# A fused decoder layer on one core: one hand-written order for everything after the last score tile

## What is computed

```python
x = _layernorm(x + _L0_attn_ref(x, ...), axis=-1)
x = _layernorm(x + _L0_xattn_ref(x, ctx_768, ...), axis=-1)
x = _layernorm(x + _L0_ffn_ref(x, ...), axis=-1)
...
# attention: rms norm and rope on q and k, tanh cap of 50, causal softmax, 16 heads on 4 kv heads
scores = jnp.tanh(scores.astype(jnp.float32) / CAP) * CAP
...
# second sublayer: attention over 32 context rows, a film, a long convolution, a film, a feed-forward, a norm
c_t = jnp.einsum('btg,bgd->btd', attn_mean, V)
y = jnp.fft.irfft(xf * Kf.T[None], n=n, axis=1)[:, :L]
h = jax.nn.gelu(h @ W1 + b1, approximate=False) @ W2 + b2
...
# third: two shared experts for all tokens, and the two best of eight by a router
shared = shared.mean(axis=0)
topk_vals, topk_idx = jax.lax.top_k(gates, TOP_K)
moe = jnp.einsum('te,etd->td', w, y)
return (shared + moe).reshape(B, L, D)
```

## Time and profile before

| | us |
|---|---|
| median of 3 runs | 712.1 (711.7 to 712.75) |
| the profiled execution's own time | 709.74 |
| its span, first to last instruction | 707.9 |
| TensorE busy | 479.5, 68% of the span |
| VectorE / ScalarE / GpSimd busy | 341.3 / 329.7 / 249.9 |
| score tiles end | about 392 |
| first scatter of batch 1 issued | 428.5 |
| first transposed block of group 1 | 616.55 |

### The profile page before, as it was taken

The page is one execution under the profiler, slowest core; times in us unless marked ns, Lnnn a source line. Parts: engine busy times, 40 slices in busy tenths (PEclk is TensorE's granted clock), DMA queues, the critical chain, the costliest instruction groups (busy, mean ns, idle before and its releaser), DMA issues.

```text
span 707.9 us, 9570 instructions
## 1 busy us (share of the span) xinstructions
PE 479.5 (68%) x3361; PEld 336.8 (48%) x3361; DVE 341.3 (48%) x1004; ACT 329.7 (47%) x557; POOL 249.9 (35%) x298
## 2 busy tenths in 40 slices
PE   3543552477758867877568788399796679676960
PEld 2221220246326733556235566366694576466960
DVE  4887658726273464845533563313542333024224
ACT  1078685666654775565647225043052343233430
POOL 2304236412350162533431526702434535413441
PEclk9975675669588997989669889699898989888895
DMA  3600000197100000000000101625044303376642
GB/s 105 195 1 0 1 1 0 32 183 155 66 24 39 1 15 1 1 1 1 0 0 1 36 26 39 186 102 168 1 125 145 120 27 98 108 256 209 211 145 85
DMA packets 39713, 51.53 MB, mean 73 GB/s; under 512 B 8561, under 2 KB 28818, under 8 KB 39666
## 3 DMA queue, kind: packets, MB, share of 16 engines
q1 hardware_dynamic: 37170, 45.78, 22.7%
q0 software_dynamic: 2496, 5.15, 2.1%
HBM read 41.25 MB, written 13.86 MB: 78 GB/s over the span
## 4 chain that ended last, share of the span: by engine, by line
PE 40%; DVE 22%; POOL 12%; ACT 9%; issue 7%; SPq 5%; DMA 3%; POOLq 0%; DVEq 0%; ACTq 0%
PE ring_s L871 5%; SPq L436 5%; PE bank_o L690 5%; POOL expert_rows L1187 4%; PE bank_d L779 4%; PE bank_o L901 3%; PE ring_s L675 3%; PE ring_u L766 3%; ACT probs L986 2%; PE ring_u L758 2%; PE bank_r L567 2%; POOL rstd L1099 2%; PE bank_o L887 2%; ACT probs L993 2%; PE bank_d L808 2%
## 5 line engine op out<-in xcount | busy, mean ns | idle before, releaser
L986 ACT ACTIVATE probs<-ring_s 128x512 f32<-128x512 f32 (+1 forms) x192 | 94.6, 523 | 77.8 <-PE ring_s L675 76.2
L675 PE MATMUL ring_s<-qT,kT 128*128 128x512 bf16 (+3 forms) x256 | 72.4, 348 | 78.7 <-ACT probs L986 64.2
L1137 POOL TENSOR_SCALAR_AFFINE_SELECT probs<-probs 128x256 f32<-128x256 f32 (+1 forms) x96 | 51.9, 571 | 156.2 <-ACT probs L993 156.2
L1042 ACT ACTIVATE g_ring<-ring_s,w_blk 128x128 f32<-128x128 f32 x184 | 52.3, 369 | 66.4 <-PE ring_s L871 66.4
L1198 POOL DMA_INDIRECT token_pairs<-y_blk,x_blk x46 | 45.5, 988 | 102.6 <-DVE y_blk L1725 100.2
L675 PEld LDWEIGHTS ring_s<-qT,kT 128*128 128x128 bf16 x256 | 23.4, 104 | 119.6 <-ACT probs L986 87.8
L993 ACT ACTIVATE probs<-probs 128x2560 f32<-128x2560 f32 x32 | 74.8, 2336 | 2.7 <-ACT probs L986 0.4
L871 PE MATMUL ring_s<-xT_blk,w_blk 128*128 128x128 f32 x368 | 53.7, 293 | 11.8 <-DVE xT_blk L1718 7.7
L690 PE MATMUL bank_o<-probs,vv 128*32 128x128 f32 (+3 forms) x512 | 55.1, 589 | 5.4 <-POOL probs L1137 5.4
L871 PEld LDWEIGHTS ring_s<-xT_blk,w_blk 128*128 128x128 f32 x368 | 48.9, 207 | 15.2 <-issue 12.4
L1099 POOL TENSOR_TENSOR rstd<-var_eps,neg_half 128x4 f32<-128x4 f32 x24 | 24.8, 1034 | 83.6 <-DVE var_eps L1433 83.6
(11 more groups left out here) (358 smaller groups left out, 970.5 us busy)
## 6 DMA issues: line engine op xcount, KB each, us to landing
w_blk<-expert_pack SPq DMA_DIRECT2D x46, 514.0 KB, 4.7
expert_pack<-in_L_ffn_W SPq DMA_DIRECT2D x16, 256.0 KB, 9.8
expert_rows<-blank SPq DMA_DIRECT2D x6, 520.0 KB, 3.1
x_blk<-expert_rows SPq DMA_DIRECT2D x10, 260.0 KB, 4.3
y_pair<-token_pairs SPq DMA_DIRECT2D x4, 512.0 KB, 4.5
x_in<-in_x SPq DMA_DIRECT2D x4, 256.0 KB, 3.1
cosm<-in_c_cos SPq DMA_DIRECT2D x1, 1024.0 KB, 6.4
sin_fwd<-in_c_sin_fwd SPq DMA_DIRECT2D x1, 1024.0 KB, 9.2
```

What stands on the lines that cost most here:

```text
L675: last = mm(bank[:, c:c + w], kT[:, r, p // 2, P * j:P * (j + 1)], qT[:, p, P * j:SEQ], start=True, stop=True)
L986: f(probs[:, pair % PAIRS_HELD, BASE[n]:BASE[n] + WIDTH[n]], ring_s[k % 2][:, 0:WIDTH[n]], ACT.Tanh, scale=1.0 / (CAP * float(np.sqrt(np.f ...
L1042: last = f(g_ring[:, s % RING, P * n:P * (n + 1)], ring_s[s % 2][:, P * n:P * (n + 1)], ACT.Gelu, bias=w_blk[:, k % SLOTS, HID + n:HID + n ...
L1137: last = g.affine_select(out=v, in_=v, compare_op=ALU.is_ge, fill=0.0, base=0, pattern=[[0, v.shape[1]], [1, P]], channel_multiplier=-1)
```

## The change

Everything up to the last score tile keeps its order. Behind it the grid walk is replaced by one list, `DRAIN`, of 173 entries (name, batch and part, or unit number), which every engine's program walks. `UNIT_AT` is gone; the list holds the calls 0 to 42 itself, so the plain loop behind still starts at 43. Three steps are cut smaller, with the same instructions: `route` into route (to the choice) and weights, `place` into place (to rank_read) and rows (table and rows), and `scatter` into eight parts of two DMAs, of which the first keeps the waits. In the main walk the parts stand next to each other where the whole stood. The parts of scatter for batches 0 and 2 issue nothing.

```diff
--- before.py
+++ after.py
@@ -74,8 +74,8 @@
     (2, 0, 0, "dft", 7), (2, 0, 1, "spectrum"), (3, 0, 5, "x2_norm"), (3, 1, 0, "x2"), (2, 1, 0, "conv", 0),
     (2, 1, 1, "conv", 1), (2, 1, 2, "conv", 2), (2, 1, 3, "conv", 3), (2, 1, 4, "conv", 4), (2, 1, 5, "conv", 5),
     (2, 2, 0, "conv", 6), (2, 2, 1, "conv", 7), (3, 1, 1, "x2T"), (3, 1, 3, "gates"), (1, 1, 4, "yT"),
-    (3, 2, 1, "gates_exp"), (1, 2, 0, "proj"), (3, 2, 1, "route"), (1, 2, 3, "x1"), (2, 2, 4, "shape_out"),
-    (3, 2, 4, "rank"), (3, 2, 5, "place"), (3, 3, 0, "scatter"), (1, 3, 1, "x1T"), (1, 3, 3, "x_norm"), (1, 3, 2, "scores"), (1, 3, 3, "xn"),
+    (3, 2, 1, "gates_exp"), (1, 2, 0, "proj"), (3, 2, 1, "route"), (3, 2, 1, "weights"), (1, 2, 3, "x1"), (2, 2, 4, "shape_out"),
+    (3, 2, 4, "rank"), (3, 2, 5, "place"), (3, 2, 5, "rows"), *[(3, 3, 0, "scatter", n) for n in range(8)], (1, 3, 1, "x1T"), (1, 3, 3, "x_norm"), (1, 3, 2, "scores"), (1, 3, 3, "xn"),
     (-1, *XT_AT, "xT"), (2, 3, 4, "h_norm"), (1, 3, 3, "cross_exp"), (-1, *QKV_AT, "qkv"), (2, 4, 1, "h"),
     (1, 4, 1, "soften"), (1, 4, 3, "attnT"), (2, 4, 4, "hT"), (-1, 5, 2, "rms"), (2, 5, 0, "up", 0),
     (2, 5, 1, "up", 1), (2, 5, 2, "up", 2), (2, 5, 3, "up", 3), (-1, 5, 2, "rope"), (2, 5, 1, "gelu"),
@@ -122,11 +122,31 @@
 SHARED = [s for s, u in enumerate(UNITS) if u[0] == "s"]
 BACK = 3
 POSITIONS = len(UNITS) + BACK
-UNIT_AT = [(B, p, n) for p in range(2, NPAIR) for n in range(NF)][2:2 + 6 * HC]
-UNIT_AT += [(B + 1, 2, 3), (B + 1, 2, 5), *[(B + 1, 3, n) for n in range(NF)], (B + 1, 7, 2), (B + 1, 7, 5)]
-UNIT_AT += [(B + 2, 0, 0), (B + 2, 0, 1)]
-UNIT_AT += [(B + 2, p, n) for p in range(3) for n in range(NF)][10:17]
-EARLY = len(UNIT_AT)
+DRAIN = [
+    ("dft", 2, 7), ("spectrum", 2), ("x2_norm", 1), ("close", 3), ("x2", 1), ("conv", 2, 0), ("tokens", 3), ("x2T", 1),
+    ("conv", 2, 1), ("gates", 1), ("gates_exp", 1), ("conv", 2, 2), ("conv", 2, 3), ("route", 1), ("unit", 0), ("yT", 3),
+    ("weights", 1), ("conv", 2, 4), ("unit", 1), ("rank", 1), ("unit", 2), ("proj", 3), ("place", 1), ("unit", 3), ("rows", 1),
+    ("x1", 3), ("conv", 2, 5), ("conv", 2, 6), ("conv", 2, 7), ("unit", 4), ("scatter", 1, 0), ("unit", 5), ("shape_out", 2),
+    ("x1T", 3), ("unit", 6), ("x_norm", 3), ("scores", 3), ("xn", 3), ("unit", 7), ("cross_exp", 3), ("h_norm", 2), ("unit", 8),
+    ("soften", 3), ("h", 2), ("unit", 9), ("unit", 10), ("scatter", 1, 1), ("scatter", 1, 2), ("attnT", 3), ("unit", 11),
+    ("hT", 2), ("unit", 12), ("up", 2, 0), ("scatter", 1, 3), ("scatter", 1, 4), ("up", 2, 1), ("gelu", 2), ("up", 2, 2),
+    ("up", 2, 3), ("down", 2, 0), ("scatter", 1, 5), ("film", 3, 0), ("film", 3, 1), ("film", 3, 2), ("film", 3, 3),
+    ("scatter", 1, 6), ("down", 2, 1), ("modulate", 3), ("down", 2, 2), ("down", 2, 3), ("scatter", 1, 7), ("dft", 3, 0),
+    ("ff_out", 2), ("dft", 3, 1), ("ffT", 2), ("ff_norm", 2), ("unit", 13), ("dft", 3, 2), ("dft", 3, 3), ("dft", 3, 4),
+    ("x2_norm", 2), ("dft", 3, 5), ("dft", 3, 6), ("unit", 14), ("dft", 3, 7), ("unit", 15), ("spectrum", 3), ("unit", 16),
+    ("conv", 3, 0), ("conv", 3, 1), ("x2", 2), ("conv", 3, 2), ("x2T", 2), ("conv", 3, 3), ("gates", 2), ("conv", 3, 4),
+    ("conv", 3, 5), ("gates_exp", 2), ("conv", 3, 6), ("route", 2), ("conv", 3, 7), ("shape_out", 3), ("unit", 17), ("weights", 2),
+    ("h_norm", 3), ("unit", 18), ("h", 3), ("unit", 19), ("rank", 2), ("place", 2), ("unit", 20), ("hT", 3), ("rows", 2),
+    ("unit", 21), ("up", 3, 0), ("unit", 22), ("up", 3, 1), ("gelu", 3), ("up", 3, 2), ("scatter", 2, 0), ("up", 3, 3),
+    ("down", 3, 0), ("scatter", 2, 1), ("down", 3, 1), ("down", 3, 2), ("down", 3, 3), ("scatter", 2, 2), ("ff_out", 3),
+    ("scatter", 2, 3), ("unit", 23), ("ffT", 3), ("unit", 24), ("ff_norm", 3), ("unit", 25), ("scatter", 2, 4), ("unit", 26),
+    ("x2_norm", 3), ("unit", 27), ("x2", 3), ("unit", 28), ("x2T", 3), ("unit", 29), ("gates", 3), ("gates_exp", 3), ("unit", 30),
+    ("route", 3), ("unit", 31), ("weights", 3), ("unit", 32), ("scatter", 2, 5), ("rank", 3), ("place", 3), ("unit", 33),
+    ("rows", 3), ("scatter", 2, 6), ("scatter", 2, 7), ("scatter", 3, 0), ("unit", 34), ("unit", 35), ("scatter", 3, 1),
+    ("unit", 36), ("unit", 37), ("unit", 38), ("unit", 39), ("scatter", 3, 2), ("unit", 40), ("unit", 41), ("scatter", 3, 3),
+    ("scatter", 3, 4), ("scatter", 3, 5), ("scatter", 3, 6), ("scatter", 3, 7), ("unit", 42),
+]
+EARLY = sum(name == "unit" for name, *_ in DRAIN)
 FINAL_AT = {BLOCKS[NB] + 4: 0, BLOCKS[NB] + 9: 1}
 STORE_BEFORE = {NB + 12: 0, NB + 17: 1}
 
@@ -156,10 +176,6 @@
         if (q, m) == (p, n) and 0 <= b < B and name in parts:
             parts[name](b, *part)
 
-    for k, at in enumerate(UNIT_AT):
-        if at == (i, p, n) and "unit" in parts:
-            parts["unit"](k)
-
 
 def iterate(parts, first, fill, close, tokens):
 
@@ -167,18 +183,23 @@
                        ("fold3",), ("fold4",), ("rope", 0), ("parts", 0), ("steps",)):
         if name in parts:
             parts[name](*row)
-    for i in range(B + 3):
-        if i < B:
-            first(i)
+    for i in range(B):
+        first(i)
         for p in range(NPAIR):
             for n in range(NF):
-                if i < B:
-                    fill(i, p, n)
-                if n == TOKENS_AT and i <= B:
+                fill(i, p, n)
+                if n == TOKENS_AT:
                     tokens(i, p)
                 run(parts, i, p, n)
-            if i <= B:
-                close(i, p)
+            close(i, p)
+
+    for name, *which in DRAIN:
+        if name == "close":
+            close(B, 0)
+        elif name == "tokens":
+            tokens(B, 1)
+        elif name in parts:
+            parts[name](*which)
 
 
 def build(nc, t, out):
@@ -1176,16 +1197,16 @@
                     last = g.tensor_copy(x_rows[:, k, NT * (b % GB):NT * (b % GB + 1), 0:D], x2[:, b, :].rearrange("p (j d) -> p j d", j=NT))
                 last.then_inc(rows_copied, 1)
 
-            def scatter(b):
+            def scatter(b, j):
 
                 if b % GB < GB - 1:
                     return
-                pool.wait_ge(blanked, 16 * GROUPS * FILL_TURNS)
-                pool.wait_ge(rows_ready, b // GB + 1)
-                for j in range(GB * NT):
-                    for k in range(2):
-                        g.indirect_dma_start(out=rows_dram, out_offset=bass.IndirectOffsetOnAxis(ap=rows_i[:, k, j:j + 1], axis=0),
-                                             in_=x_rows[:, k, j, :], in_offset=None).then_inc(scattered[b // GB], 16)
+                if j == 0:
+                    pool.wait_ge(blanked, 16 * GROUPS * FILL_TURNS)
+                    pool.wait_ge(rows_ready, b // GB + 1)
+                for k in range(2):
+                    g.indirect_dma_start(out=rows_dram, out_offset=bass.IndirectOffsetOnAxis(ap=rows_i[:, k, j:j + 1], axis=0),
+                                         in_=x_rows[:, k, j, :], in_offset=None).then_inc(scattered[b // GB], 16)
 
             def unit(at):
                 s = at - BACK
@@ -1648,6 +1669,10 @@
                 one(tt(cmp_a[:, :, :, :], cmp_a[:, :, :, :], cmp_b[:, :, :, :], ALU.add))
                 one(v.tensor_reduce(chosen, cmp_a[:, :, :, :], AX, ALU.add))
                 ts(chosen_bf[:, :, :], chosen, 2.0, None, ALU.is_lt).then_inc(chosen_ready, 1)
+
+            def weights(b):
+
+                chosen, w_tok = of_batch(chosen_g, b), of_batch(w_tok_g, b)
                 dve.wait_ge(chosen_ready, b + 1)
                 one(ts(chosen, chosen, 2.0, None, ALU.is_lt))
                 dve.wait_ge(gates_exp, b + 1)
@@ -1665,6 +1690,9 @@
                        held[:, :].unsqueeze(1).broadcast_to([P, NT, NE]), ALU.add))
                 op(ts(wT[0:NT * NE, b, :], bank_r[0:NT * NE, P:2 * P], float(NSH), None, ALU.mult))
                 tt(held[:, :], held[:, :], bank_r[:, 64 + NT * NE:64 + NT * NE + NE], ALU.add).then_inc(rank_read, 1)
+
+            def rows(b):
+
                 if b % GB == GB - 1:
                     dve.wait_ge(rank_read, b + 1)
                     block_table(b // GB)
@@ -1767,7 +1795,7 @@
                      "proj": proj, "scores": scores, "x_norm": x_norm, "soften": soften, "film": film_step,
                      "modulate": modulate, "spectrum": spectrum, "shape_out": shape_out, "hT": hT_step,
                      "ffT": ffT_step, "ff_norm": ff_norm, "x2": x2_step, "gates": gates_step,
-                     "route": route, "place": place, "unit": unit, "x1": x1_step, "xn": xn_step,
+                     "route": route, "weights": weights, "place": place, "rows": rows, "unit": unit, "x1": x1_step, "xn": xn_step,
                      "h_norm": h_norm, "h": h_step, "x2_norm": x2_norm}, first, nothing, close, tokens)
             moe()
 
```

## The result

The changed kernel takes 678.3 us in the median of four executions (674.9 to 679.9), the kernel before 712.1: a ratio of 0.953, interval 0.950 to 0.956. Forecast were 671.5 and a range of 652 to 694. The profiled execution took 677.41 with a span of 675.6, so 1.8 lie around it, as before.

The account below looks back on a forecast made before the run. TensorE's waits, 51.5 us between 394.2 and 616.55, bound that stretch, not throughput. Group 1's first matmul comes 39.1 earlier, clock gives 1.5: span 667.3, plus 1.84 around it and 2.36 to the median: 671.5 us, range 652 to 694.

Parts of the forecast that it names:

- case C: Rival: the list packs better than reckoned, most waits and their slow clock halve: 659 us; chance 0.17.
- Item 3: VectorE makes the row table ahead of x1(3), outlasting TensorE's work beside it: a new wait of 2.1 us.
- Item 4: Only two scatter DMAs precede batch 2's norm on GpSimd: 1.0 us left of 12.3; the other 14 cost nothing.
- Item 6: Batch 3's spectrum stands behind batch 2's second norm on VectorE: TensorE waits 2.5 us, before it was 5.0.
- Item 9: Batch 3's rows step on VectorE now stands between block units 33 and 34: TensorE waits 3.1 us.
- Item 10: Batch 3's scatter shares GpSimd with y scatters of units 34 to 41; the third y buffer is late twice: 2.0 us.
- The clock: TensorE's slow clock after three waits that pass 2 us, beside the first wait: 2.4 us each, 7.2 together.
- The scatter's path: From the end of batch 3's rows to unit 55's first matmul: 42.3 us, ending at 583.5, against 582.2 on TensorE's path.
- The rule against the change: VectorE beside the chunked scatter may lock GpSimd out: up to 8 us, time up to 679; the sum took 0.
- B: Rival: the chains of batches 2 and 3 (spectrum, h norm, output norm) keep their waits: 688 us; chance 0.23.
- D: Rival: the list only moves waits and the time stays near 712 us; chance 0.03.
- E: Rival: slower, as block units wait for the three y buffers; 718 us if landing plus queue is 10.5; chance 0.07.

Follow-up runs that it names:

- e1: The changed kernel run once more, unaltered, beside the kernel before: 660.46 us, ratio 0.927.
- e12: The changed kernel with batch 1's last three scatter chunks behind batch 2's feed-forward norm, and batch 2's second norm behind batch 3's spectrum: 672.21 us.
- e6: The kernel before, order kept, with only batch 1's scatter cut into eight chunks: 717.39 us, ratio 1.010 to the kernel before.

## Why the prediction was right or wrong

**The result as a whole.** 678.3 stands in the forecast's own case, 662 to 681, 6.8 above its middle; on the chip of e1 the kernel is 11.0 below it, in case C. So the middle was hit by neither. The forecast had one number for a kernel that has two, by chip. That the first measurement fell into the forecast's own case is in part luck: without late starts the sum is 11.0 too high, and the late starts, which it doesn't have, add 17.9.

**The sum.** Unit 55's transpose was forecast at 580.3 = 394.2 + 156.3 + 22.6 + 7.2. On the chip of e1 it comes at 572.6: its waits add up to 17.2, 5.4 less, and TensorE is busy 161.0 from 394.2 on, so 4.7 of slow clock, 2.5 less. In the first measurement it comes at 590.2: waits 28.6, 6.0 more, busy 167.1, so 10.8 of slow clock, 3.6 more. Both shares of slow clock are what is left when 156.3 is taken off, so they can't confirm it. By the granted clock e1 lost about 3.4 us (next but one paragraph), so 1.3 of its 161.0 is not placed: the constant held to about that.

**Item by item,** e1 first, then the first measurement where it differs. Item 1 (values): 5.2 forecast, 5.2. Item 2: 0.7, measured 0.3. Item 3 (rows ahead of x1): 2.1, measured 0.35. The row table took 4.7 us in e1 (from the block counts at 417.85 to 422.55), as the second of the two in the earlier trace rows did, and I had taken the first, 6.3. That is 1.6 of the 1.75 us. Item 4 (hT of batch 2): 1.0, measured 0.4, and the 14 remaining DMAs hidden, as said; e12 shows with how little to spare. Item 5: 0.5, nothing. Item 6 (spectrum): 2.5, measured 1.8, and 5.2 where the add of ffT starts late. Item 7: 1.0, measured 0.5 + 0.2. Item 8 (output norm beside blocks): 4.5, measured 0.7 + 1.7 + 0.8 + 1.1 = 4.3. Item 9 (rows of batch 3): 3.1, measured 3.45. Item 10 (y ring): 2.0, measured 0; in the first measurement 1.2, behind a late start. So items 3, 6 and 10 are most of what was mis-sized, 4.5 of the 5.4 us, all in one direction: where I could not see a queue's slack I wrote a small wait. (Two waits of 0.3, at 406.08 and 432.50, are in no item.) Item 10 was also where rule and row differed. The Trainium skill, "DMA: Bandwidth & Descriptors", section "Anatomy of one DMA — SWDGE (gpsimd) path", gives 2.15 as an estimate and so no wait. The row itself was read too simply: the view of token_pairs mixes the y scatters with the loads of y_pair, and the view of y_blk, which has the scatters alone, gives 2.2/3.8/5.1 before the change. In e1 the last landing report of a y scatter comes 2.2 to 5.7 us after its issue, 4.1 in the median of 46, and there was no wait all the same. So the skill's page would have given the right wait, by a landing that only the shortest of these come near. What kept the third buffer free was not traced; VectorE must come back to it later than I had it.

**The clock.** I charged three waits with 2.4 each. Apart from the values' stretch (0.51 from 399.7 to 404.3 in e1, 0.56 before), two stretches of e1 have a granted clock under 1: 0.87 from 467 to 480, behind the spectrum's 1.8, and 0.79 from 533 to 541, behind the 3.45 at rows. The block unit behind rows takes 3.6 us instead of 1.9, so 1.7 lost, and the inverse transforms behind the spectrum lose as much. So the price of 2.4 was some 0.7 too high, and the third wait (item 3) wasn't there.

**The scatter's path.** Rows(3) was done 0.7 ahead of the first scatter DMA, at 537.9 in the first measurement (541.2 forecast) and at 533.5 in e1. From there to unit 55's matmul e1 took 575.15 - 533.5 = 41.7, where I had 42.3. In e1 the weights behind that path do hold TensorE by 0.4 (the first block's have landed at 575.06, the matmul starts at 575.15), so the two paths are as near to each other as the forecast said.

**The step that failed** is the last sentence of the forecast: "a step on a queue that I took as free, ScalarE's above all, which I found nowhere last". In the first measurement four shared units between 560.63 and 578.26 take 17.6 us instead of 4 x 1.75 = 7.0, for ScalarE, 10.6 us, and the late add costs 3.4 in front of the spectrum, with some slow clock behind it. But it is not ScalarE's queue that is full. Its activations are released late, in and at the end of GpSimd's runs of indirect DMAs. The trace of the kernel before gave no sign of it, but it could hardly have: it is of an execution that is none of the four above, and by its landing reports (last section) it looks like those of the lower level. e6, in the old order on a chip of the higher level, does have late starts, at batch 3's scatter.

**The rule against the change** did not decide. The Trainium skill, "SBUF — State Buffer", section "Who interferes with whom", would lock GpSimd out beside VectorE. The 32 scatter DMAs of the new order have a median of 0.96 us and a longest of 1.27; before it was 1.22. The 8 us that stood as a bound are not there, and the trace shows nothing of the rule.

**The rivals.** B (the chains keep their waits): no, the 4.4 and 5.8 went to 0.3 and 0.9. It holds for the spectrum alone, and only with late starts. C: its time came, 660.5 for 659, on the chip of e1, but not by halves: items 2 to 9 fell from 15.4 to 11.3 and the clock from 7.2 to 4.7. Of the 11.0 under my forecast 8.4 are unit 55's matmul (575.15 for 583.5), and 2.4 what I had added from the profiled execution to the median, which was 0.0 there. D and E: no; y_blk never waited more than 1.2.

**What each part is worth.** On the chip of e1: the whole list 51 us; without the chunks of batch 1, 34; without the early scatter of batch 3, 42. And e6, on a chip of the higher level, shows the chunks to be worth nothing, or less, in the old order. So two thirds of the gain come without the chunks of batch 1, and the chunks are worth their 17 only inside the list: chunks let the norm past, the list gives TensorE other work until the rows have landed.
